# A two-layer transformer in one kernel: the first feed-forward's weights are dequantised inside the first attention

## The chip, the cores and the metric

The kernel runs on one core of a Trainium2 chip. The time is device microseconds of one execution. A core has TensorE (in the rows PE for matmuls, PEld for the loads of its stationary operand), VectorE (DVE), ScalarE (ACT), GpSimd (POOL) and SyncE (SP, which only issues transfers here), and 16 DMA engines. Each engine runs its own instructions in order; engines wait for each other by semaphores.

## The reference

Two layers, each an attention and a feed-forward, each followed by a residual addition and a layer norm. The sizes of layer 0, which the change touches:

- The input is 4 sequences of 256 tokens, 512 wide.
- Attention with latents: 32 heads; query latents of 192 (`c_q = h @ w_q_down`), key/value latents of 64, a rotated part of 64 per head. `q_lat = c_q @ w_q_up_nope @ w_uk` per head, scores from 64 latent and 64 rotated features, causal softmax, `out = probs @ c_kv @ w_uv`, then `@ w_out`.
- A feed-forward whose weights come in 4 bits, eight to a 32-bit word, with a zero and a scale for each group of 128 rows:

```python
def _dequant(qw, qz, sc, g_idx):
    wq = (qw[:, None, :] >> shifts) & 15            # 512 x 2752 and 1376 x 512 weights
    zq = ((qz[:, :, None] >> shifts) & 15) + 1.0    # 4 and 10 groups
    return sc[g_idx] * (wq - zq[g_idx])
h = silu(x @ w_gate) * (x @ w_up);  y = h @ w_d
```

Layer 1 has a grouped-query attention beside a latent one, and a feed-forward whose weights are quantised and dequantised by a 16-value code. The change leaves it alone.

## The kernel before

Everything is float32. A product is made of three matmuls of rounded parts (`product`: high x high, high x low, low x high; lines 63 to 65), so every operand is split into a high part (a rounding copy, mostly on ScalarE) and a low part (a subtraction, on VectorE or GpSimd).

The kernel is a row of blocks: `l0_attention_block`, `gptq_block` (which dequantises), `ffn_block`, and the same for layer 1. The order of the work in each engine's queue is written out by hand.

**First attention.** Four groups of 8 heads; a group is 16 steps, a step is one pair of heads of one sequence. Step n on TensorE: `scores(n)`; a query unit ("A", n+2) that makes the query features of the step after next; `apply(n-2)` (probabilities times values); `turn(n-1, 0)` (transposes); `output(n-3)`; `turn(n-1, 1)`; and in some steps a further unit: ("B", n) in steps 0 to 3 folds `w_uv` with `w_out`, ("W", n-12) in steps 12 to 15 folds the next group's `w_q_up_nope` with `w_uk`. Units write into a ring of two PSUM banks; `ring_free` counts those that have been emptied. The 192 query latents lie as 128 rows and 64 rows, so a query unit is, for each of two heads, three matmuls of 128 rows and three of 64 rows, 256 columns each (`project`, line 546).

Step n on VectorE: `peaks(n)` (the rows' maxima of the scores, line 766), `rotate` (lines 746 to 748), `shares` (the reciprocals, line 772), `probs_low(n-1, 0)` (line 777), `out_low(n-2)` (line 782), `probs_low(n-1, 1)`, in every fourth step `add_output` (line 790), and `plain_low` (line 758) for the B or W unit. ScalarE runs the exponentials, the scaling by the shares and the high parts; GpSimd adds the two halves of the rotation (line 366), splits the raw weights of the coming units (lines 351 and 359: two pieces in steps 0, 1, 2 and 15, one in 10 to 13) and makes the queries' low part (line 374). SyncE loads the raw weight pieces into two buffers, each once the split has freed it. Groups 1 and 2 are one loop body (`Fori`); groups 0 and 3 are written out.

**`gptq_block`.** After the attention, SyncE loads packed words, zeros, scales and group indices. VectorE makes one-hot tables of the group indices, unpacks the zeros and splits the scales (lines 1782 to 1805). Then 35 pieces of up to 512 columns: TensorE spreads zeros and scales over the rows with three matmuls, and VectorE shifts and masks the words (line 1816), subtracts the zeros (1821) and multiplies by the scales (1824) into `WGU` and `WD`, which stay in SBUF.

**`ffn_block`.** 22 units (11 tiles of the hidden width, twice for two halves of the tokens); ScalarE and GpSimd split each unit's weights from `WGU` and `WD`, TensorE multiplies.

Of the kernel before, what the change touches and what calls it, by code (L numbers as in the profile page):

```python
# [10 lines left out]
I32 = mybir.dt.int32  # L11
# [15 lines left out]
INTER = 1376  # L27
FT = 11
# [159 lines left out]
def l0_step_units(n, last):  # L188
# [8 lines left out]
    return out  # L197


def l0_units(first, last):  # L200

    out = [("W", i, 0) for i in range(PAIRS)] + [("A", 0), ("A", 1)] if first else []
    for n in range(L0_STEPS):
        out += l0_step_units(n, last)
    return out


def l0_attention_block(nc, x, X, XT, CQ, KC, CV, signals, norm, normed, ident, ident_d, banks, w_down, lat_cos_d, lat_sin_d,
                       w_nr, w_ou, cos_d, sin_d, mask_d):

    NP = 2
    with ExitStack() as ctx:
# [5 lines left out]
        QW = pair("qw", [P, PAIRS, NP, 2, P])  # L218
# [7 lines left out]
        mask = sb("mask", [P, P], F32)  # L226
        mask_r, ident_r = sb("mask_r", [P, P], R32), sb("ident_r", [P, P], R32)
        straight, crossed = sb("straight", [P, 2, HALF], F32), sb("crossed", [P, 2, HALF], F32)
        probs = sb("probs", [P, 2, NP * 3 * P], F32)
        dip, total, share = sb("dip", [P, 2, 4], F32), sb("total", [P, 2, 4], F32), sb("share", [P, 2, 4], F32)  # L230
        LN = QL + LAT + ROPE
        lat_raw, lat_w = sb("lat_raw", [P, KT, LN], F32), pair("lat_w", [P, KT, LN])
        lat_cos, lat_sin = sb("lat_cos", [P, SEQ], F32), sb("lat_sin", [P, SEQ], F32)
        lat_straight, lat_cross = sb("lat_straight", [P, 2, HALF], F32), sb("lat_cross", [P, 2, HALF], F32)
# [11 lines left out]
        lat_low, lat_ready = sem("lat_low"), sem("lat_ready")  # L246
        passed = {"pool": sem("passed_pool")}
        landed = [sem("landed0"), sem("landed1")]
        split_hi, split = sem("split_hi"), sem("split")
# [15 lines left out]
        def span(kind, first, last, g):  # L265

            lists = {"pieces": lambda f, l: [x for _, x in l0_pieces(f, l)], "units": l0_units,
                     "roped": lambda f, l: [u for u in l0_units(f, l) if u[0] == "A"],
                     "plain": lambda f, l: [u for u in l0_units(f, l) if u[0] in "WB"]}[kind]
            n0, n1 = len(lists(True, False)), len(lists(False, False))  # L270
            base = 0 if first else n0 + n1 * (g - 1)
            odd = 0 if first else n0
            names = lists(first, last)
            return {x: base + i for i, x in enumerate(names)}, {x: odd + i for i, x in enumerate(names)}

        assert len(l0_pieces(False, False)) % 2 == 0 and len(l0_units(False, False)) % 2 == 0
# [7 lines left out]
        def plain_cells(name, bank, x):  # L284

            i = name[1]
            if name[0] == "W":
                view = bank[:, 0:4 * LAT].rearrange("p (k h r) -> p k h r", k=2, h=NP)
                return [(x[0][:, i, :, 0, 0:LAT], view[:, 0]), (x[0][0:QP, i, :, 1, 0:LAT], view[0:QP, 1])]
            return [(x[1][:, i, :], bank[:, :])]  # L290
# [4 lines left out]
        def _(sp):  # L295
            sp.dma_start(ident[:, :], ident_d).then_inc(ident_landed, 16)
            for i in range(TT // 2):
                sp.dma_start(X[:, 2 * i:2 * i + 2, :], x[2 * i * P:2 * (i + 1) * P, :]
                             .rearrange("(t p) d -> p t d", p=P)).then_inc(x_landed[i], 16)
                if i == 0:  # L300
                    sp.dma_start(lat_raw[:, :, :], w_down.rearrange("(k p) m -> p k m", p=P)).then_inc(lat_landed, 16)
            sp.dma_start(lat_cos[:, :], lat_cos_d).then_inc(lat_landed, 16)
            sp.dma_start(lat_sin[:, :], lat_sin_d).then_inc(lat_landed, 16)
            sp.dma_start(cos[:, :], cos_d).then_inc(tables, 16)
            sp.dma_start(sin[:, :], sin_d).then_inc(tables, 16)
            sp.dma_start(mask[:, :], mask_d).then_inc(tables, 16)

            def body(g, first, last):
                at, place = span("pieces", first, last, g)
                for _, name in l0_pieces(first, last):  # L310
                    kind, i, h, ahead = name
                    slot = place[name] % 2
                    wait(sp, split, at[name] - 1)
                    if kind == "NR":
# [1739 lines left out]
```

## Time and profile before

| | |
|---|---|
| median of 3 runs | 2554.64 us (2553.92 to 2555.03) |
| the profiled execution | 2551.88 us, its span 2550.0 us |
| mean granted TensorE clock | 0.959 of 2.4 GHz |
| busy: TensorE, weight loads, VectorE, ScalarE, GpSimd | 92%, 80%, 69%, 57%, 62% of the span |
| first attention, its steps | 60 to 590 us |
| dequantisation | 590 to 685 us |
| first feed-forward | 685 to 885 us |

The span runs from the first to the last instruction. Busy shares are means over stages of different kinds, so the rows below go by stretches: length, then for each engine the busy time and (x) its instructions, then the granted clock (1.00 is 2.4 GHz, 0.50 is 1.2 GHz). A time line gives start, duration, engine, line, operation, output<-input, shape and count; in brackets is the idle time before it and what ended it.

### The profile page before, as it was taken

The page shows a single profiled execution, that of the slowest core. Times are in us where ns is not written, and L with a number is a line of the kernel's source. Part 1 is how long each engine was busy: PE and PEld are TensorE (multiplying, and loading weights), DVE is VectorE, ACT ScalarE, POOL GpSimd, SP SyncE. Part 2 cuts the span into 40 slices and gives each one's busy share as a digit, 9 for nine tenths or more (in the row PEclk, how much of TensorE's full clock was granted, in tenths as well). Part 3 has the DMA queues.
Part 4 walks back from the last instruction along what each step waited for, and adds up shares of the span by engine and source line. Part 5 has one row for each costly group of instructions (what it writes and reads, how often), then busy time and mean ns, then how long its engine had stood idle before and what let it go on. Part 6 is the DMA issues. An engine that isn't in the chain of part 4 may idle for free. (4 is left out here: it accounts for less than half of the span.)

```text
span 2550.0 us, 44356 instructions
## 1 busy us (share of the span) xinstructions
PE 2338.2 (92%) x14245; PEld 2027.7 (80%) x14245; DVE 1770.5 (69%) x3131; ACT 1459.0 (57%) x3978; POOL 1572.4 (62%) x1320
## 2 busy tenths in 40 slices
PE   7999999983899889999999999999999999987998
PEld 5788888872588778888888888888888888875886
DVE  4666666666823379888888888888888888972232
ACT  2666656660133347766666666676676766664432
POOL 3555555620154377877887878878878878751442
PEclk8999999995599999999999999999999999998999
DMA  2101110101000120110111111101101111003000
GB/s 97 32 28 36 28 36 23 29 1 41 1 1 1 35 67 29 52 54 16 56 45 37 52 38 48 51 19 57 50 24 56 37 47 48 18 5 141 1 17 17
DMA packets 41349, 93.70 MB, mean 37 GB/s; under 512 B 4836, under 2 KB 6760, under 8 KB 39808
## 3 DMA queue, kind: packets, MB, share of 16 engines
q1 hardware_dynamic: 41092, 90.55, 11.1%
q8 instruction: 128, 2.10, 0.4%
q14 instruction: 129, 1.06, 0.1%
HBM read 79.78 MB, written 10.75 MB: 36 GB/s over the span
## 5 line engine op out<-in xcount | busy, mean ns | idle before, releaser
L1129 POOL TENSOR_TENSOR a_nf_acc<-a_nf_acc,a_nf_term 128x512 f32<-128x512 f32 (+1 forms) x416 | 591.3, 1421 | 140.5 <-ACT a_nf_term L1223 70.1
L1609 POOL TENSOR_TENSOR f_w_lo<-WGU,f_w_hi 128x512 fp32r<-128x512 f32 x88 | 114.8, 1307 | 345.4 <-ACT f_w_hi L1625 345.2
L1183 ACT ACTIVATE a_probs<-bank,a_dip 128x128 f32<-128x128 f32 (+1 forms) x512 | 208.3, 419 | 191.5 <-DVE a_dip L1464 191.5
L1192 ACT ACTIVATE a_probs<-a_probs,a_share 128x128 f32<-128x128 f32 (+1 forms) x512 | 192.5, 464 | 68.7 <-DVE a_share L1470 68.7
L1110 POOL TENSOR_TENSOR a_qk_lo<-a_straight,a_qk_hi 128x512 fp32r<-128x512 f32 (+1 forms) x160 | 194.4, 1217 | 41.2 <-ACT a_qk_hi L1169 41.2
L63 PE MATMUL bank<-a_wo_hi,a_ot_hi 128*128 128x512 f32 x512 | 212.3, 415 | 0.0
L1475 DVE TENSOR_TENSOR a_pt_lo<-bank,a_pt_hi 128x384 fp32r<-128x384 f32 x256 | 140.8, 550 | 90.7 <-ACT a_pt_hi L1200 90.0
L1534 DVE TENSOR_SCALAR a_nf_term<-a_nf_unit 128x512 f32<-128x512 f32 (+1 forms) x288 | 199.7, 738 | 3.4 <-DVE a_nf_unit L1517 0.8
L65 PE MATMUL bank<-a_wo_hi,a_ot_lo 128*128 128x512 f32 x512 | 201.2, 393 | 0.0
L64 PE MATMUL bank<-a_wo_lo,a_ot_hi 128*128 128x512 f32 x512 | 200.8, 392 | 0.0
L1169 ACT ACTIVATE a_qk_hi<-a_straight 128x512 fp32r<-128x512 f32 (+1 forms) x160 | 94.4, 590 | 183.2 <-DVE a_straight L1449 183.2
L366 POOL TENSOR_TENSOR a_straight<-a_straight,a_crossed 128x512 f32<-128x512 f32 x64 | 82.5, 1289 | 182.6 <-DVE a_crossed L748 182.6
L1675 DVE TENSOR_TENSOR f_hidden<-bank,f_act_gate 128x512 f32<-128x512 f32 x44 | 30.4, 692 | 231.5 <-PE bank L65 213.8
L1338 PE MATMUL bank<-ident,a_probs 128*128 128x128 f32 x768 | 133.8, 284 | 52.5 <-DVE a_pt_lo L1475 52.5
L443 ACT ACTIVATE a_probs<-bank,a_dip 128x128 f32<-128x128 f32 (+1 forms) x256 | 104.2, 419 | 133.3 <-DVE a_dip L766 133.3
L63 PE MATMUL bank<-a_wvk_hi,XT_hi 128*128 128x320 f32 x512 | 170.8, 334 | 7.6 <-DVE a_crossed L1446 7.6
L1449 DVE TENSOR_TENSOR a_straight<-a_straight,a_crossed 128x512 f32<-128x512 f32 (+1 forms) x160 | 156.8, 980 | 5.5
L64 PE MATMUL bank<-a_wvk_lo,XT_hi 128*128 128x320 f32 x512 | 159.6, 312 | 0.0
L65 PE MATMUL bank<-a_wvk_hi,XT_lo 128*128 128x320 f32 x512 | 159.5, 312 | 0.0
L1338 PEld LDWEIGHTS bank<-ident,a_probs 128*128 128x128 f32 x768 | 85.4, 142 | 86.7 <-DVE a_pt_lo L1475 78.4
L63 PE MATMUL bank<-a_pt_hi,a_vl_hi 128*128 128x256 f32 (+1 forms) x512 | 137.8, 269 | 11.2 <-DVE a_pt_lo L1475 10.9
L63 PE MATMUL bank<-XT_hi,a_wql_hi 128*128 128x256 f32 x512 | 144.0, 281 | 0.0
(243 smaller groups left out, 8537.1 us busy)
## 6 DMA issues: line engine op xcount, KB each, us to landing
a_raw<-in_l_o SPq DMA_DIRECT2D x64, 256.0 KB, 2.7
a_raw<-in_l_vk SPq DMA_DIRECT2D x32, 384.0 KB, 3.1
a_raw<-in_l_ql SPq DMA_DIRECT2D x32, 320.0 KB, 2.9
a_raw<-in_l_ou SPq DMA_DIRECT2D x32, 288.0 KB, 2.8
n_codes<-coded_w SPq DMA_DIRECT2D x8, 1056.0 KB, 12.8
a_raw<-in_l_nr SPq DMA_DIRECT2D x16, 384.0 KB, 3.1
a_nf_raw<-in_w_nf SPq DMA_DIRECT2D x24, 256.0 KB, 2.6
coded_w<-a_nf_acc SPq DMA_DIRECT2D x24, 256.0 KB, 2.0
```

The source lines that it names most:

```text
L63: pe.matmul(out, lh, rh, start=first, stop=False)
L64: pe.matmul(out, lh, rl, start=False, stop=False)
L65: return pe.matmul(out, ll, rh, start=False, stop=last)
L1110: pool.tensor_tensor(rope_cell(name, QK.lo), src, rope_cell(name, QK.hi).bitcast(F32), ALU.subtract)\
L1129: pool.tensor_tensor(acc, left, nf_term[:, i % CODE_RING, 0:w], ALU.add).then_inc(nf_added, 1)
L1183: act.activation(probs[:, n % 2, col:col + keys], bank[:, at:at + keys], ACT.Exp, bias=dip[:, n % 2, i:i + 1], accum_out=total[:, n % 2, i ...
L1192: ins = act.activation(cell, cell, ACT.Copy, scale=share[:, n % 2, i:i + 1])
L1338: last_ = pe.transpose(TURN[:, i * P:(i + 1) * P], probs[:, n % 2, col:col + P], ident[:, :])
L1449: dve.tensor_tensor(row, row, crossed[:, 0:n], ALU.add).then_inc(rope_sum, 1)
L1475: dve.tensor_tensor(PT.lo[:, at], TURN[:, 0:3 * P], PT.hi[:, at].bitcast(F32), ALU.subtract)\
L1534: dve.tensor_scalar(nf_term[:, i % CODE_RING, 0:w], nf_unit[:, 0:w], -BOUNDS[k], JUMPS[k], ALU.is_ge, ALU.mult).then_inc(nf_terms, 1)
L1609: pool.tensor_tensor(lo, src, hi.bitcast(F32), ALU.subtract).then_inc(part_lo[i], 1)
```

## The change

- The first feed-forward's weights are dequantised inside the first attention, in 66 units of 256 columns, called ("G", i). They run from step 5 of group 0 to step 13 of group 3, one in each step, two in steps 6, 8 and 10 of groups 0 to 2. TensorE does two matmuls for a unit, with 128 rows: rows 0 to 31 hold zeros, rows 64 to 95 the scales' high part, rows 96 to 127 their low part, and two one-hot tables select zeros or scales. VectorE does shift, subtraction and multiplication at the end of its step. The result goes from one of three small buffers to DRAM.
- The preparation runs on VectorE in steps 0 to 3 of group 0, and a shift of the packed words in step 5.
- `gptq_block` is gone. `ffn_block` loads each unit's three weight tiles from DRAM; ScalarE waits for them.
- The query latents 128 to 191 lie twice in the second row block (rows 0 to 63 and 64 to 127 of it), their low part beside zeros, and the second block of the folded weight holds its high part over its low part. Two matmuls of 128 rows take the place of three of 64.
- Groups 1 and 2 are written out instead of being a loop; the loads of raw pieces are issued at stated steps.

```diff
+DEQ_WIDE, DEQ_UNITS = 44, 66
+DEQ_FIRST = 5
+DEQ_TWICE = [(g, n) for g in range(3) for n in (6, 8, 10)]
...
         def groups(eng, body):
             body(0, True, False)
-            with eng.Fori(1, L0_GROUPS - 1) as g:
+            for g in range(1, L0_GROUPS - 1):
                 body(g, False, False)
...
+            def store(i):
+                src = parked[:, i % 3, :]
+                sp.wait_ge(dequantised, i + 1)
...
+                sp.dma_start(dst, src).then_inc(q_stored[i % 3], 16)
...
+                    if first and n == 3:
+                        sp.wait_ge(q_ready, 1)
+                        sp.dma_start(packed, q["q_gu"]).then_inc(q_landed, 16)
+                        sp.dma_start(packed_d, q["q_d"]).then_inc(q_landed, 16)
+                    for _, i in dequantised_at(g, n):
+                        store(i)
...
-                            product(pe, out, QW[:, i, h, 0, :], CQ[:, 0, at], True, False)
-                            last_ = product(pe, out, QW[0:QP, i, h, 1, :], CQ[0:QP, 1, at], False, True)
+                            product(pe, out, (QW_both[:, i, h, 0, :], QW_lo[:, i, h, :]), CQ[:, 0, at], True, False)
+                            pe.matmul(out, QW_both[:, i, h, 1, :], CQ.hi[:, 1, at], start=False, stop=False)
+                            last_ = pe.matmul(out, QW_both[:, i, h, 1, :], CQ.lo[:, 1, at], start=False, stop=True)
...
+                    elif name[0] == "G":
+                        pe.wait_ge(q_ready, 1)
...
+                        pe.matmul(bank[:, 0:PART], hot_zero[:, rows:rows + P], table[:, cols:cols + PART],
+                                  start=True, stop=True)
+                        last_ = pe.matmul(bank[:, PART:2 * PART], hot_scale[:, rows:rows + P], table[:, cols:cols + PART],
+                                          start=True, stop=True)
...
+                def dequantise(names):
+                    for name in names:
...
+                        wait(dve, differed, i - 1)
+                        dve.tensor_scalar(nib[:, i % 2, :], src, shift, 15, ALU.logical_shift_right, ALU.bitwise_and)\
+                           .then_inc(nibbled, 1)
+                    for name in names:
...
+                        dve.wait_ge(nibbled, i + 1)
+                        dve.wait_ge(unit_done, number[name] + 1)
+                        wait(dve, dequantised, i - 1)
+                        dve.tensor_tensor(diff[:, i % 2, :], nib[:, i % 2, :], bank[:, 0:PART], ALU.subtract)\
+                           .then_inc(differed, 1)
+                    for name in names:
...
+                        dve.wait_ge(differed, i + 1)
+                        wait(dve, q_stored[i % 3], 16 * (i // 3))
+                        dve.tensor_tensor(parked[:, i % 3, :], diff[:, i % 2, :], bank[:, PART:2 * PART], ALU.mult)\
+                           .then_inc(dequantised, 1)
+                        dve.wait_ge(dequantised, i + 1)
+                        dve.sem_inc(ring_free, 1)
...
                     for name in units:
-                        if name[0] != "A":
+                        if name[0] in "WB":
                             plain_low(name)
+                    if first and n < 4:
+                        (zeros_out, scales_high, scales_low, groups_hot)[n]()
+                    if first and n == DEQ_FIRST:
+                        odd_words_shifted()
+                    dequantise([name for name in units if name[0] == "G"])
...
+                if source and u < FT:
+                    act.wait_ge(loaded[u], 48)
...
+            if source:
+                for m in range(FT):
+                    for i in range(2):
+                        sp.dma_start(WGU[:, :, (i * FT + m) * P:(i * FT + m + 1) * P], source[0][i * FT + m])\
+                          .then_inc(loaded[m], 16)
+                    sp.dma_start(WD[:, m, :], source[1][m]).then_inc(loaded[m], 16)
...
-def gptq_block(nc, ident, banks, WGU, WD, q):
```

`zeros_out`, `scales_high`, `scales_low`, `groups_hot` and `odd_words_shifted` hold the instructions of the old block's preparation (the zeros' shifts; copies and the plus one; the scales' low part; two pairs of one-hot tables; the shifts of the packed words), over 32 to 128 partitions, each set closed by a wait for its own end.

## Rows read from the trace of the kernel before

**Rows 1.** Busy time by stretch: length, PE, PEld, DVE, ACT, POOL, PEclk, DMA, GB/s.
```profile
60.45:187.90 127.45, 122.25 (x826) 105.91 (x826) 81.51 (x159) 81.17 (x264) 68.14 (x76) 0.97 0.09 28
187.90:318.90 131.00, 128.32 (x874) 109.98 (x873) 84.52 (x164) 82.72 (x268) 74.60 (x85) 1.00 0.12 34
318.90:450.47 131.57, 131.56 (x874) 112.91 (x874) 84.53 (x165) 82.83 (x268) 68.31 (x76) 0.97 0.10 28
450.47:589.84 139.37, 128.33 (x834) 109.81 (x832) 88.95 (x176) 82.72 (x264) 53.11 (x57) 0.96 0.05 14
589.84:690.70 100.86, 57.86 (x121) 31.81 (x122) 83.26 (x155) 4.20 (x9) 2.63 (x3) 0.51 0.08 26
690.70:885.00 194.30, 188.58 (x828) 152.75 (x828) 54.67 (x89) 72.08 (x122) 83.00 (x64) 1.00 0.03 8
```

**Rows 2.** Time line at the entry of the first feed-forward: start, duration, engine, instruction.
```profile
685.60 0.63 ACT L1625 ACTIVATE f_w_hi<-WGU 128x512 fp32r<-128x512 f32 x1 [100.38 <-PEq L1733]
...
690.70 0.50 PE L63 MATMUL bank<-XT_hi,f_w_hi 128*128 128x512 f32 x1 [1.41 <-DVE XT_lo L145]
```

**Rows 3.** DMA issues of the page: count, size, median time to landing.
```profile
a_raw<-in_l_o SPq DMA_DIRECT2D x64, 256.0 KB, 2.7
```

**Rows 4.** Time line of TensorE in a plain step of group 1.
```profile
252.37 0.28 PE L63 MATMUL bank<-CQ_hi,a_qw_hi 128*128 128x256 f32 x1
...
252.61 0.28 PE L65 MATMUL bank<-CQ_hi,a_qw_lo 128*128 128x256 f32 x1
...
252.82 0.38 PE L63 MATMUL bank<-CQ_hi,a_qw_hi 64*128 64x256 f32 x1
...
254.46 0.38 PE L63 MATMUL bank<-a_pt_hi,CV_hi 128*128 128x256 f32 x1
...
259.74 0.28 PE L63 MATMUL bank<-CQ_hi,a_qw_hi 128*128 128x256 f32 x1
```

**Rows 5.** Time line of VectorE in the late step of group 3.
```profile
509.28 0.99 DVE L766 TENSOR_REDUCE a_dip<-bank 128x2 f32<-128x256 f32 x2
...
514.54 0.56 DVE L777 TENSOR_TENSOR a_pt_lo<-bank,a_pt_hi 128x384 fp32r<-128x384 f32 x1 [0.95 <-ACT a_pt_hi L460]
```

**Rows 6.** Time line of VectorE: two shifts of 256-column pieces.
```profile
661.81 0.29 DVE L1816 TENSOR_SCALAR q_nib<-q_packed 128x256 uint32<-128x256 uint32 x1
...
662.92 0.28 DVE L1816 TENSOR_SCALAR q_nib<-q_packed 128x256 uint32<-128x256 uint32 x1
```

**Rows 7.** Time line of VectorE and GpSimd behind the probabilities' low part.
```profile
204.57 0.69 DVE L758 TENSOR_TENSOR a_bh_lo<-bank,a_bh_hi 128x512 fp32r<-128x512 f32 x1 [0.74 <-ACT a_bh_hi L433]
...
305.29 0.56 DVE L777 TENSOR_TENSOR a_pt_lo<-bank,a_pt_hi 128x384 fp32r<-128x384 f32 x1 [1.01 <-ACT a_pt_hi L460]
305.76 1.28 DVE L790 TENSOR_TENSOR X<-bank,X 128x512 f32<-128x512 f32 x2
305.85 1.29 POOL L374 TENSOR_TENSOR a_q_lo<-a_straight,a_q_hi 128x512 fp32r<-128x512 f32 x1 [1.54 <-ACT a_q_hi L428]
306.96 0.47 DVE L758 TENSOR_TENSOR a_qw_lo<-bank,a_qw_hi 128x128 fp32r<-128x128 f32 x2
```

**Rows 8.** Busy time in the preparation of the dequantisation, columns as in rows 1.
```profile
606.09:625.06 18.97, 1.54 (x4) 1.24 (x5) 18.69 (x39) 0.00 (x0) 0.00 (x0) 0.50 0.00 0
```

**Rows 9.** Time line of GpSimd and VectorE, then one tile's instruction (min/median/max) and its group.
```profile
18.36 1.27 POOL L359 TENSOR_TENSOR a_wn_lo<-a_raw,a_wn_hi 128x512 fp32r<-128x512 f32 x1
18.41 1.30 DVE L695 CAST a_mask_r<-a_mask 128x128 fp32r<-128x128 f32 x1
...
L1534 DVE TENSOR_SCALAR a_nf_term<-a_nf_unit x288: 411/454/1983, 919.3 to 2290.4; 128x512 f32<-128x512 f32 x112, 128x576 f32<-128x576 f32 x32
...
L1534 DVE TENSOR_SCALAR a_nf_term<-a_nf_unit 128x512 f32<-128x512 f32 (+1 forms) x288 | 199.7, 738 | 3.4 <-DVE a_nf_unit L1517 0.8
```

**Rows 10.** TensorE at the loop's jump back, then the stretch behind it.
```profile
316.51 0.32 PE L63 MATMUL bank<-KC_hi,a_q_hi 128*128 128x128 f32 x1 [2.63 <-issue]
...
319.00:322.00 3.00, 3.00 (x12) 2.33 (x10) 0.92 (x2) 1.72 (x8) 0.00 (x0) 0.50 0.23 81
```

More of the change, by code:

```diff
@@ L27 @@
 INTER = 1376
+Q_GROUPS = (D // 128, INTER // 128)
 FT = 11
@@ L265, in span, with plain_cells @@
         def span(kind, first, last, g):
[L267 to L276, printed above, removed]
+            names = {"pieces": lambda k: [x for _, x in l0_pieces(k == 0, k == L0_GROUPS - 1)], "units": l0_units,
+                     "tails": lambda k: [x for _, x in l0_pieces(k == 0, k == L0_GROUPS - 1) if x[0] == "NR"],
+                     "roped": lambda k: [u for u in l0_units(k) if u[0] == "A"],
+                     "plain": lambda k: [u for u in l0_units(k) if u[0] in "WB"]}[kind]
+            base = sum(len(names(k)) for k in range(g))
+            at = {x: base + i for i, x in enumerate(names(g))}
+            return at, at
         def groups(eng, body):
             body(0, True, False)
-            with eng.Fori(1, L0_GROUPS - 1) as g:
+            for g in range(1, L0_GROUPS - 1):
                 body(g, False, False)
             body(L0_GROUPS - 1, False, True)
-        def plain_cells(name, bank, x):
+        def plain_cells(name, bank):
             i = name[1]
@@ L328, in body @@
                 number, _ = span("units", first, last, g)
+                tails, _ = span("tails", first, last, g)
                 def split_piece(name):
@@ L389, in body @@
                 for n in range(L0_STEPS):
-                    own = [name for name in l0_step_units(n, last) if name[0] == "A"]
+                    own = [name for name in l0_step_units(g, n) if name[0] == "A"]
                     for name in own:
@@ L541, in piece_ready @@
                     else:
-                        names = [x for _, x in l0_pieces(False, False)]
-                        left = len(names) - names.index((kind, i, h, 1))
-                        pe.wait_ge(split, pieces[("OU", 1, 0, 0)] - left + 1)
+                        pe.wait_ge(split, span("pieces", g == 1, False, g - 1)[0][(kind, i, h, 1)] + 1)
                 def project(name):
@@ L650, in body @@
                     scores(n)
-                    units = l0_step_units(n, last)
+                    units = l0_step_units(g, n)
                     for name in units:
@@ L804, in body @@
                 for n in range(L0_STEPS):
-                    units = l0_step_units(n, last)
+                    units = l0_step_units(g, n)
                     peaks(n)
@@ L1588, in ffn_block @@
         UNITS = 2 * FT
+        loaded = [sem(f"loaded{m}") for m in range(FT)] if source else None
         late = range(TT - 2, TT)
```

377 lines of the change are left out of this document (205 added, 172 removed).

## The prediction

> **What bounds the kernel now.** I read the sums by stretch first [rows 1]. The first attention runs in four head groups of 16 steps. TensorE is busy 122 to 132 us in each of them (VectorE 82 to 89), and its clock is at 2.4 GHz (granted 0.96 to 1.00). So TensorE sets the time there. The fifth stretch, 100.86 us long, is the dequantisation. There VectorE is busy 83 us and the clock is at 1.2 GHz (0.51). The time line of the two ends of that stretch gives its price [rows 2]: the attention's last addition ends at 589.84, and the first product with a dequantised weight starts at 690.70. Then I followed one step on TensorE [rows 4], one step in which VectorE came late [rows 5], and the dequantisation of a 256-column piece [rows 6], because these decide what a step costs once pieces are in it.
>
> **The removed stage.** 100.86 us go. In their place the feed-forward must fetch its first three weight tiles (256 KB each, issued 0.3 to 0.5 us apart). A 256 KB load of this kernel lands after 2.7 us [rows 3]; written in 512-byte pieces I take 3.5, so about 4.7 us until ScalarE may start. From its first weight copy to the first product were 5.1 us (685.60 to 690.70 [rows 2]); TensorE's transposes are done by then, so I take 4.7. Sum 9.4. Before, the clock was back at 1.00 there [rows 1]; after a wait of this length it will start at 1.2 GHz, and a first stretch like the one at 319 to 322 (0.50) [rows 10] costs some 2.3 us. 100.9 - 11.7 = **89.2 us saved**. Every further load has a unit of 8.8 us to arrive in (22 units in the 195 us to 885 [rows 1]), so it is hidden.
>
> **TensorE in a step.** A plain step takes 7.37 us (252.37 to 259.74), of which the query unit takes 2.09 [rows 4]. Its matmuls stand 0.12 apart (two spacings from 252.37 to 252.61), but a change between 128 and 64 rows costs more: the first 64-row one starts 0.21 behind 252.61, and the one behind it is late as well. Twelve spacings would be 1.44, so the four changes take the other 0.65. Ten matmuls of 128 rows take 1.20, and 0.10 behind the last change goes too. The dequantisation unit adds two matmuls, 0.24. Without the register-addressed loop the plain step was 7.29 already (groups 0 and 3). New: 7.29 - 0.89 - 0.10 + 0.24 = **6.54 us**. If TensorE stayed the bound, 64 steps would give back some 45 us.
>
> **VectorE in a step.** It won't stay the bound. VectorE's queue is in order, and a step is a chain through ScalarE and back. The late step shows it with no wait for TensorE [rows 5]: maxima at 509.28, second half of the probabilities' low part at 514.54, 5.26 later, and after another 0.48 the queue is free (305.29 to 305.76 [rows 7]): 5.74 us. In other steps the rotation waited about 1 us longer for the query unit; the shorter unit takes that wait away. Behind the chain now comes the dequantisation: three instructions of 0.29, 0.42 and 0.42 us, 1.11 from one piece's start to the next [rows 6], and 0.11 for the wait that now stands behind the multiplication: **1.22 us**, in line before the next maxima. So a plain step is 6.96, VectorE's and not TensorE's. Two units cost 2.0. Every fourth step adds 1.20 for the residual (305.76 to 306.96 [rows 7]). A step with an output-weight unit waits for ScalarE and ends its low part at 7.23 (it starts 0.56 + 0.74 = 1.30 us behind the probabilities' start [rows 7]; 0.05 for the ring and 0.62 for itself), in all 8.45; one with a folded query weight 7.8.
>
> A middle group: steps 0 to 3 are 3 x 8.45 + 8.78 = 34.1; steps 4 to 11 are 13.9 + 8.95 + 7.2 + 7.75 + 7.2 + 8.95 + 7.2 = 61.2; steps 12 to 15 are 3 x 7.8 + 8.55 = 31.95. Sum **127.2**, against 131.0 and 131.6 [rows 1]. Half of that difference is the loop's jump back, which goes: TensorE idled 2.63 us at 316.51 and then ran at 1.2 GHz [rows 10]. So -3.8 and -4.4. Group 3 by the same step prices over its first 14 steps: 109.2 against 110.2, **-1.0**; its tail has no units.
>
> **Group 0** carries the preparation. Before it ran from 606.09 to 625.06 on VectorE, 19.0 us [rows 8]; with a second pair of one-hot tables (1.4) and three tail shifts (1.4) it is 22 us: 3.6, 3.9, 3.7 and 7.8 in steps 0 to 3 and 3.0 in step 5. VectorE's slack there is 1.2 to 1.5 per step, so steps 0 to 3 get longer by 2.2, 2.0, 2.9 and 6.4, steps 4 and 5 together by 2.0, and steps 6 to 15 by 2.3 in sum (the unit prices above against the old lengths): 17.8. TensorE idles several us at a time here, more than the 2.63 us before the drop of rows 10, and comes back at 1.2 GHz: +2. The packed words (2.4 MB) are asked for at the end of step 3 and needed 12 us later. The old stage began its preparation 16.2 us after its own start, with all its loads landed before [rows 1, 8]; a wait of a few us here is in the range, none is in the sum. The lead-in gains 1 us by two shorter query units. **+19**.
>
> **A price that hides in no instruction's own length.** The shift reads and writes SBUF at two elements a cycle's worth (0.285 us for 256 columns). A copy of that kind, 128x128, took 1.30 us at 18.41, exactly as long as GpSimd's subtraction from 18.36 was running, and TENSOR_SCALAR of 128x512 in the second attention, which has GpSimd working beside it nearly all the time, averages 0.738 (0.411 to 1.983, median 0.454) [rows 9]. So a shift can cost 0 to 1.29 us more (one whole GpSimd subtraction); the mean of that row lies 0.33 above its least. I go through the step: GpSimd splits weights behind the rotation in steps 0 to 2, 10 to 13 and 15 and is caught in the middle of an instruction (0.4 to 0.5 each, 19 steps with units); in two-unit steps the second shift loses its turn; in plain steps the shift would stand where the residual starts at 305.76, 0.09 ahead of GpSimd's query subtraction at 305.85 [rows 7]. Taken 66 x 0.30 = **+20**, and +4 for the preparation, whose copies are of the same kind.
>
> That GpSimd and VectorE exclude one another is a rule of the Trainium skill (SBUF — State Buffer, "Who interferes with whom"): whoever issues first holds the shared port pair for its whole instruction, and the other blocks. By that rule the 0.09 us in the plain steps decide; the trace agrees in the copy of rows 9.
>
> **Sum.** -89.2 - 3.8 - 4.4 - 1.0 + 19 + 24 = -55.4. The profiled execution took 2551.88 (span 2550.0 and 1.9 around it), so 2496.5; the median of the runs is 2.8 above it: **2499 us**. Stores of the results (128 KB each, three buffers, so three steps for some 2.5 us) and SP's queue, in which each store stands behind the loads of its step, I cost at nothing: the next load needs that step's split anyway. If that cover went, a load would come up to a step late, some 3 us in each of 8 pairs.
>
> **Rivals.**
> A. The shift loses its race in the plain steps too, and waits out the 1.29 us less the lead: 21 steps by some 1.15 us more, +24: 2523. For: only 0.09 us of lead. Against: ScalarE's order fixes it, and a late ScalarE only helps. 0.20.
> B. No port price: -24: 2475. For: half of the instructions in the tile's row take no more than 0.454, GpSimd or not. Against: the copy in the same rows. 0.17.
> C. VectorE's work fits in its idle time (1.0 us waiting for ScalarE in each step before the second low part [rows 5]), and TensorE stays the bound: groups shorter by 12, 12, 12 and 8 more, no port price: 2431. Against: the dequantisation stands behind that wait, not in it. 0.06.
> D. Slower: TensorE's idle time between steps brings the clock down to 1.2 GHz within the attention. Its 6.54 us of work become some 13, a step grows by 5 to 6 us, and from 10 such steps of 64 the 55 us are eaten; all of them give some 2850. For: after 2.63 us of idling it fell [rows 10]. Against: the new gaps are 0.4 us in plain steps, and TensorE's clock was 1.00 in the first middle group (busy 128.3 of 131.0 [rows 1]). 0.03.
>
> **Numbers.** My forecast 0.54 (2485 to 2512 by itself), the rivals as given. Range 2465 to 2530: it holds B and A and leaves out C and D and a preparation that costs much more. What this measurement can tell from no change is 0.2%, 5 us: faster 0.96, same 0.01, slower 0.03.
>
> **What would show it.** Right: no idle 100 us; VectorE without idle before its maxima, TensorE waiting 0.3 to 0.5 us a step; plain steps near 7.0; step 3 of group 0 near 15; shifts of 0.28 beside some of 0.7 to 1.5. Wrong: plain steps at 6.5 (C) or 8.1 (A), a granted clock near 0.5 in groups 1 to 3 (D), a first product later than 15 us behind the last addition.

## The result and the profile after

| | before | changed |
|---|---|---|
| median (4 runs each on one chip) | 2554.28 us (2550.14 to 2555.03) | 2517.30 us (2512.97 to 2518.66) |
| profiled execution, its span | 2551.88, 2550.0 | 2517.41, 2515.6 |
| mean granted TensorE clock | 0.959 | 0.962 |

The ratio is 0.9856 (95% interval 0.9839 to 0.9873): 37 us faster, where 55 were forecast. The time by stretch (the four groups, the entry of the feed-forward), columns as in [rows 1]:

```profile
58.51:223.50 164.99, 124.94 (x820) 114.42 (x819) 126.11 (x245) 79.06 (x264) 76.75 (x82) 0.84 0.15 47
223.50:359.58 136.08, 120.68 (x878) 109.28 (x878) 106.91 (x221) 79.61 (x268) 72.97 (x85) 0.97 0.17 48
359.58:495.77 136.19, 121.06 (x878) 109.89 (x878) 106.98 (x221) 79.86 (x268) 73.03 (x85) 0.97 0.17 48
495.77:640.89 145.12, 124.46 (x834) 111.83 (x834) 103.08 (x218) 80.81 (x264) 53.09 (x55) 0.93 0.09 27
640.89:651.31 10.42, 2.98 (x16) 2.61 (x17) 4.30 (x10) 3.98 (x9) 2.74 (x3) 0.56 0.83 247
```

Beside [rows 1]: the 100.86 us stretch has become one of 10.42; group 0 is 37.5 us longer, groups 1 and 2 are 5.1 and 4.6, group 3 with its tail 5.8. TensorE is busy for less time than before in groups 1 to 3 (120.7 us against 128.3 in group 1) and idles 15 us in a middle group; VectorE is busy 22 us more there.

VectorE and GpSimd at the end of a plain step (what was [rows 7]). The shift starts 0.09 us ahead of GpSimd's subtraction and takes 0.28. The subtraction and the multiplication behind it run beside that GpSimd instruction and take their usual 0.42:

```profile
271.29 0.56 DVE L929 TENSOR_TENSOR a_pt_lo<-bank,a_pt_hi 128x384 fp32r<-128x384 f32 x1 [0.94 <-ACT a_pt_hi L545]
271.76 0.28 DVE L950 TENSOR_SCALAR a_lat_in<-a_q_wide 128x256 uint32<-128x256 uint32 x1
272.08 0.42 DVE L958 TENSOR_TENSOR a_lat_in<-a_lat_in,bank 128x256 f32<-128x256 uint32 x1
272.54 0.42 DVE L965 TENSOR_TENSOR a_lat_in<-a_lat_in,bank 128x256 f32<-128x256 f32 x1
273.10 0.42 DVE L918 TENSOR_REDUCE a_dip<-bank 128x2 f32<-128x256 f32 x1
...
271.85 1.34 POOL L453 TENSOR_TENSOR a_q_lo<-a_straight,a_q_hi 128x512 fp32r<-128x512 f32 x1 [1.46 <-ACT a_q_hi L510]
```

Two-unit step 10 of group 1, VectorE, GpSimd and TensorE. The two shifts take 2.13 us and end when the second of GpSimd's instructions does (within 0.15 us): both are waited out (such a wait is called a lock below). TensorE stands 3.48 us at the first matmul of the next query unit, whose ring bank the first multiplication empties:

```profile
312.64 2.13 DVE L950 TENSOR_SCALAR a_lat_in<-a_q_wide 128x256 uint32<-128x256 uint32 x2
...
312.09 1.26 POOL L438 TENSOR_TENSOR a_wn_lo<-a_raw,a_wn_hi 128x512 fp32r<-128x512 f32 x1
313.31 1.31 POOL L453 TENSOR_TENSOR a_q_lo<-a_straight,a_q_hi 128x512 fp32r<-128x512 f32 x1
...
315.88 0.58 PE L64 MATMUL bank<-CQ_hi,a_qw_both 128*128 128x256 f32 x1 [3.48 <-DVEq L968]
```

The sums by stretch of a plain step, of step 10 and of step 11. In step 11 the clock is 0.75, TensorE is busy throughout, and the step takes 9.82 us:

```profile
266.00:273.10 7.10, 6.68 (x52) 6.08 (x52) 5.67 (x12) 4.72 (x16) 2.63 (x3) 1.00 0.07 21
...
305.68:316.54 10.86, 6.95 (x50) 6.14 (x50) 9.29 (x17) 4.72 (x16) 5.77 (x8) 0.91 0.17 52
316.54:326.36 9.82, 9.82 (x62) 9.43 (x62) 6.51 (x12) 4.87 (x16) 5.60 (x7) 0.75 0.12 32
```

Group 0, steps 0 to 3, in the same view; then VectorE and TensorE in them. In steps 0 to 2 VectorE idles 2 us and more for ScalarE's copy of the output weight, and only then do the preparation's instructions come; TensorE idles up to 10.86 us, and its clock is 0.65 to 0.74 (1.00 in step 3):

```profile
58.51:72.66 14.15, 7.30 (x43) 6.65 (x42) 10.27 (x32) 4.22 (x14) 7.47 (x10) 0.74 0.15 43
72.66:86.60 13.94, 9.09 (x48) 8.27 (x48) 10.06 (x13) 5.20 (x16) 8.80 (x10) 0.65 0.16 43
86.60:99.44 12.84, 8.71 (x49) 8.13 (x49) 9.24 (x13) 5.48 (x17) 9.43 (x10) 0.73 0.10 31
99.44:114.80 15.36, 9.38 (x62) 7.95 (x60) 12.98 (x21) 5.36 (x17) 3.67 (x3) 1.00 0.09 27
```

```profile
76.67 0.90 PE L697 MATMUL bank<-ident,a_probs 128*128 128x128 f32 x3 [10.86 <-DVE a_pt_lo L929]
...
80.79 0.69 DVE L910 TENSOR_TENSOR a_bh_lo<-bank,a_bh_hi 128x512 fp32r<-128x512 f32 x1 [2.11 <-ACT a_bh_hi L515]
81.40 1.73 DVE L854 TENSOR_SCALAR XT_hi<-a_q_wide 32x2816 fp32r<-32x2816 uint32 x1
```

The entry of the feed-forward (what was [rows 2]): last addition, first weight copy, first product.

```profile
639.60 1.29 DVE L975 TENSOR_TENSOR X<-bank,X 128x512 f32<-128x512 f32 x2
...
647.33 0.63 ACT L1818 ACTIVATE f_w_hi<-WGU 128x512 fp32r<-128x512 f32 x1 [11.06 <-DMA WD<-deq_d]
...
651.31 0.79 PE L64 MATMUL bank<-XT_hi,f_w_hi 128*128 128x512 f32 x1 [7.13 <-DVE XT_lo L146]
```

### The profile page after: what moved, and what is told of

It is laid out like the page before. It is cut to its first block and busy times, and to the rows that moved or that the text cites. A ratio compares the mean times of both kernels' runs of the same rounds, so it can differ in the third digit from the quotient of the medians.

```text
span 2515.6 us, 43939 instructions
## 1 busy us (share of the span) xinstructions
PE 2265.2 (90%) x14144; PEld 2008.6 (80%) x14144; DVE 1791.2 (71%) x3230; ACT 1450.9 (58%) x3980; POOL 1585.0 (63%) x1336
## 5 line engine op out<-in xcount | busy, mean ns | idle before, releaser
L64 PE MATMUL bank<-XT_hi,f_w_hi 128*128 128x512 f32 x352 | 140.1, 398 | 9.4 <-DVE XT_lo L146 9.4
```

Of the source, the lines that this page charges most:

```text
L64: pe.matmul(out, lh, rh, start=first, stop=False)
```

## The experiments

Each was timed beside the kernel before, and the ratio is to that; a difference between two of the new kernels is taken from their ratios (0.0010 is 2.55 us), since they ran beside different runs of before. A step's length below is the distance between the starts of VectorE's first maxima of two steps. Here are the steps of group 1, in the changed kernel and in the three others that tell most. Group 2 of the changed kernel has the same sum, but 8.09 in step 9 and 8.89 in step 11:

| step | 0 | 1 | 2 | 3 | 4 | 5 | 6 | 7 | 8 | 9 | 10 | 11 | 12 | 13 | 14 | 15 | sum |
|---|---|---|---|---|---|---|---|---|---|---|---|---|---|---|---|---|---|
| before, unrolled | 8.67 | 8.65 | 8.67 | 8.67 | 7.29 | 7.29 | 8.03 | 6.54 | 7.29 | 7.27 | 8.04 | 6.53 | 8.31 | 8.30 | 8.42 | 8.18 | 126.2 |
| changed | 9.24 | 8.63 | 8.89 | 8.63 | 7.11 | 7.10 | 9.26 | 7.11 | 9.11 | 7.10 | 10.86 | 9.82 | 8.10 | 8.11 | 8.91 | 8.10 | 136.1 |
| early shift | 8.83 | 8.31 | 8.57 | 8.31 | 6.78 | 6.80 | 8.81 | 6.78 | 7.65 | 6.78 | 8.82 | 6.78 | 7.79 | 7.79 | 8.61 | 7.77 | 125.2 |
| no VectorE work | 8.10 | 8.10 | 8.10 | 8.27 | 6.72 | 6.71 | 7.71 | 6.76 | 6.95 | 6.72 | 7.71 | 6.77 | 7.73 | 7.72 | 8.07 | 7.83 | 120.0 |

**The shift, moved forward** (`shift_early`).

```diff
                         out_low(n - 2)
+                    nibbles(deq)        # the shifts of this step's units; step 5 of group 0 as before
                     probs_low(n - 1, 1)
...
                     dequantise(deq)     # subtraction and multiplication
```

> The shift of a unit's words stands ahead of the probabilities' second low part, where VectorE idles 0.94 us in a plain step (270.35 to 271.29 in the trace after), and no longer at the step's end. Theory Q (VectorE's queue at the end of a step sets its length, and a shift caught behind a GpSimd instruction is paid there, then again as TensorE's wait for the ring and as a lower clock): plain steps 7.10 -> 6.8, the two-unit step 8 9.11 -> 7.9, step 10 10.86 -> 9.0, step 11 9.82 -> 7.4; total 2475 to 2485. Rival L (only the 0.28 us of the shift itself leaves the queue, locks cost nothing behind themselves): 66 x 0.30 = 20, total 2497. Rival M (GpSimd's rotation sum and splits run in just that gap, so the shift is caught there, delays the low part and TensorE's transposes): 2517 or more.

Measured: 2479.17 us (2475.36 to 2481.50), ratio to before 0.9723 (0.9706 to 0.9739), 34 us below the changed kernel; from trace to trace the attention ends 39.2 us earlier (last addition's start 600.45 against 639.60). The steps are those forecast by theory Q within 0.25 us but for step 11, which gained more (6.78). Here are the shifts of the two-unit step 8 of group 1, in VectorE's idle time ahead of the low part, for 0.50 us together. They start 0.14 us before GpSimd's rotation sum ends (277.71 for 1.28), so there is next to nothing to wait out:

```profile
278.85 0.50 DVE L950 TENSOR_SCALAR a_lat_in<-a_q_wide 128x256 uint32<-128x256 uint32 x2
279.90 0.56 DVE L929 TENSOR_TENSOR a_pt_lo<-bank,a_pt_hi 128x384 fp32r<-128x384 f32 x1 [0.54 <-ACT a_pt_hi L545]
```

Moving an instruction of 0.28 us was worth 34 to 39 us over 65 places (the shift in step 5 of group 0 stayed): 0.32 us in a plain step, 1.46 in step 8, and 5.1 in steps 10 and 11 together, where the lock, the long wait for the ring and the lower clock went with it. Rival L's 20 us, the instruction's own length, are the larger part of that; the rest is priced by the kernels that follow. Rival M falls: the longest shift is now 0.70 us.

**Is it the port?** Two kernels put another instruction of 256 columns in the shift's place. First `shift_one_port`:

```diff
-  dve.tensor_scalar(nib, src, shift, 15, logical_shift_right, bitwise_and)
+  dve.tensor_tensor(nib, same, same, subtract)     # same: 256 columns of SBUF
```

> In the place of the shift stands a TENSOR_TENSOR subtraction of 256 float32 columns, SBUF to SBUF (it leaves out the unpacking of the weights). By the trace such an instruction takes 0.42 us, not 0.28. Theory P (the long shifts of 1.0 to 1.6 us are the port shared with GpSimd, held by GpSimd's whole instruction, and two-input instructions don't wait for it): all 66 take 0.4 to 0.45 us, none over 0.6; plain steps 7.10 -> 7.24, step 8 9.11 -> 8.4, step 10 10.86 -> 9.3, step 11 9.82 -> 8.0; 10 us of excess go, 9 us of length come, and TensorE's stall and clock in steps 10 and 11 give 5 to 10: total 2507 to 2513. Rival R (they were late for a reason other than the port, such as the SBUF traffic of GpSimd or DMA): instructions of over 1 us stay in steps 8 to 11, total 2525 or more.

Measured: 2528.34 us, ratio 0.9915 (0.9898 to 0.9931). The times are the rival's, and long instructions stayed. But the test didn't tell the two causes apart: P took it that an instruction with two SBUF inputs doesn't wait, and that could be wrong by itself. The second kernel, `shift_from_psum`, reads PSUM instead:

```diff
+  dve.tensor_scalar(nib, bank[:, 0:PART], 1.0, None, mult)     # bank: PSUM
```

> The changed kernel, order as it is; in the place of the shift stands a one-input TENSOR_SCALAR of 256 columns that reads the unit's zeros from PSUM and writes SBUF (it leaves out the unpacking; the weights become zeros). Theory P (a VectorE instruction waits for GpSimd's when it needs the SBUF port that they share; both the shift, SBUF to SBUF in one input, and the two-input SBUF subtraction tried earlier, with its longest at 1.50, need it; one that reads PSUM does not): all 66 take about 0.42 us, none over 0.6; plain steps 7.10 -> 7.24, step 8 9.11 -> 8.4, step 10 10.86 -> 9.4, step 11 9.82 -> 8.0 or less: total 2507 to 2513. Rival R (any VectorE instruction that starts while GpSimd is inside one is late, or its write is what waits): some stay over 1 us, as 1.50 in the SBUF subtraction, total 2525 to 2530 like that one.

Measured: 2514.23 us, ratio 0.9857 (0.9840 to 0.9873). All 66 instructions of each kernel by tile (min/median/max ns): the changed kernel's shifts in two rows and its subtraction (one input in SBUF, one in PSUM), then the SBUF subtraction, then the PSUM copy:

```profile
L950 DVE TENSOR_SCALAR a_lat_in<-a_q_wide x44: 280/294/1372, 133.1 to 431.6; 128x256 uint32<-128x256 uint32 x44
L950 DVE TENSOR_SCALAR a_lat_in<-a_lat_turn x22: 261/285/1346, 441.5 to 610.0; 128x256 uint32<-128x256 uint32 x22
L958 DVE TENSOR_TENSOR a_lat_in<-a_lat_in,bank x66: 405/421/423, 133.4 to 610.3; 128x256 f32<-128x256 uint32 x66
```

```profile
L951 DVE TENSOR_TENSOR a_lat_in<-XT_hi x66: 391/418/1502, 132.4 to 619.6; 128x256 f32<-128x256 f32 x66
```

```profile
L951 DVE TENSOR_SCALAR a_lat_in<-bank x66: 407/415/425, 133.0 to 606.4; 128x256 f32<-128x256 f32 x66
```

In the same place, beside the same GpSimd instructions, reading PSUM leaves no long one. So what waits is an instruction all of whose inputs lie in SBUF, one input or two. A read from SBUF alone isn't enough: the subtraction in line 958 has one input there and one in PSUM, often runs beside GpSimd, and never took more than 0.423 us. The Trainium skill (SBUF — State Buffer, "Who interferes with whom") names two kinds of VectorE instruction that exclude GpSimd's: those in a 2-port mode, which `tensor_scalar` can enter, and those with two SBUF inputs, these only against a GpSimd instruction that reads SBUF; these runs agree (0.425 us at most from PSUM, 1.37 and 1.50 from SBUF). Steps 8, 10 and 11 of group 1 went to 8.28, 9.48 and 7.23, within 0.1 us of P's forecast or below it; the total is 1 us above P's range and far below R's. Over all 66 the instruction is 0.13 us longer (8.6 us), and the attention ends 3.5 us earlier all the same (last addition's start 636.09 against 639.60). So the locks on the shifts had cost some 12 us, 11.0 of it in the shifts' own lengths (44 at a mean of 0.480 and 22 at 0.398 make 29.9 us; 66 at 0.285 would be 18.8). Of the 34 us that the early shift brought, then, some 12 are locks and most of the rest is the shift's own length, gone from the end of the queue.

**No VectorE work in the units** (`no_vector_work`).

With a memset of the buffers in step 5, and in each unit:

```diff
-  shift, subtraction, multiplication
+  dve.wait_ge(unit_done, number[name] + 1)
+  dve.memset(nib[0:1, i % 2, 0:1], 0).then_inc(dequantised, 1)
```

> Units keep TensorE's two matmuls and the store; VectorE's shift, subtraction and multiplication are left out (the weights are zeros), one memset of an element stands for them; the preparation stays. Theory Q (VectorE's queue is the bound of nearly all steps with units): plain steps 7.10 -> 6.7 (TensorE's 6.68 of work), steps 6, 8, 10 and 11 to 6.8 to 7.0, TensorE's clock 1.00 throughout groups 1 to 3; groups 1 and 2 some 117 to 119 us each (from 136), group 3 some 8 us shorter, group 0 some 14: total 2455 to 2465. Rival T (TensorE or ScalarE bounds the steps, units are nearly hidden): above 2500.

Measured: 2460.50 us, ratio 0.9649 (0.9632 to 0.9666); groups 1 and 2 take 120.0 each (117 to 119 expected), a plain step 6.72 with TensorE busy for 6.68 of it:

```profile
241.85:248.57 6.72, 6.68 (x52) 6.08 (x51) 4.73 (x11) 4.76 (x16) 1.87 (x2) 1.00 0.06 20
```

VectorE's part of the units cost the changed kernel 53 us, 34 of them by the place of the shift. Rival C of the prediction would have needed all of this to be hidden, and even this kernel is 29 us above its 2431.

**The query unit with 64 rows again**, on the changed kernel (`rows64`) and on that with the early shift (`rows64_early`):

```diff
-  pe.matmul(out, QW_both[:, i, h, 1, :], CQ.hi[:, 1, at], ...)
-  last_ = pe.matmul(out, QW_both[:, i, h, 1, :], CQ.lo[:, 1, at], ...)
+  three matmuls on rows 0 to 63: (QW_both, CQ.hi), (QW_both, CQ.lo), (QW_both, CQ.hi)
```

> The query unit's second row block goes back to three matmuls of 64 rows (the third repeats the first's operands, so the weights' low part is left out there). Theory Q: TensorE's work in a plain step goes from 6.68 to some 7.5 us and it becomes the bound there: plain steps 7.10 -> 7.5; steps 6, 8, 10 and 11, where VectorE is 2 us late, keep their length; over 60 steps some 15 to 25 us: total 2532 to 2542. Rival S (TensorE has enough idle time in every step, the rows' change bought nothing): 2517 to 2522. Rival F (the full 0.99 us in each of 64 steps): 2580.

> The kernel with the early shift, with the query unit's second row block in three matmuls of 64 rows again (the third repeats the first's operands). Theory Q (now that VectorE's queue is short, TensorE's longer step shows in full in plain steps, and without the clock's drops of the run on the changed kernel, since its long stalls for the ring are gone): plain steps 6.78 -> 7.52, step 8 7.65 -> 7.9, steps 0 to 3 and 12 to 15 +0.4 to 0.7; some 8 to 9 us a group: total 2510 to 2515. Rival C (the 43 us that the 64 rows cost on the changed kernel were mostly clock drops behind two-unit steps, and these return): above 2520, with steps 7, 9 and 11 over 9 us.

Measured: 2560.36 us, ratio 1.0046 (1.0030 to 1.0063), and 2537.99, ratio 0.9934 (0.9912 to 0.9956). Both lie above theory Q, though its plain steps came out (7.45 to 7.53), and the first fits none of its rivals. Of the second run's rival C the total and steps 7 and 11 hold (11.75 and 10.21 in group 1); step 9 stayed at 7.48. Step 6 (two units) and step 7 of group 1, first with 64 rows and the early shift, then the early shift alone:

```profile
276.31:285.85 9.54, 8.03 (x54) 6.99 (x54) 7.81 (x17) 4.95 (x16) 2.93 (x3) 0.97 0.06 16
285.85:297.61 11.76, 11.76 (x54) 10.17 (x52) 5.67 (x13) 4.98 (x16) 2.19 (x2) 0.59 0.07 22
```

```profile
258.99:267.80 8.81, 7.26 (x55) 6.46 (x54) 7.64 (x17) 4.72 (x16) 2.96 (x3) 1.00 0.05 16
267.80:274.58 6.78, 6.57 (x51) 5.97 (x50) 5.58 (x13) 4.72 (x16) 2.21 (x2) 1.00 0.14 41
```

In both TensorE had stood for the ring late in step 6 (1.5 and 1.43 us). With 128 rows it went on at 2.4 GHz (1.00); with 64 rows the next step averaged 0.59, so for most of it TensorE was at 1.2 GHz, and the step took 5 us longer. The rows alone don't decide that, nor does the stop's length alone. The changed kernel, all with 128 rows, stops for 1.73 us at the same place of groups 1 and 2, behind step 8, and step 9 then runs at 1.00 in one group and at 0.83 in the other:

```profile
297.91 0.39 PE L64 MATMUL bank<-CQ_hi,a_qw_both 128*128 128x256 f32 x1 [1.73 <-DVEq L968]
298.58:305.68 7.10, 6.87 (x54) 6.28 (x53) 5.67 (x12) 4.72 (x16) 2.53 (x2) 1.00 0.12 37
...
434.04 0.58 PE L64 MATMUL bank<-CQ_hi,a_qw_both 128*128 128x256 f32 x1 [1.73 <-DVEq L968]
434.71:442.80 8.09, 8.09 (x55) 7.70 (x55) 5.77 (x12) 4.84 (x16) 2.54 (x2) 0.83 0.12 34
```

In group 1 of the kernel with the early shift the 64 rows cost 18.1 us (143.3 against 125.2): 6.9 in steps 7 and 11 beyond the 0.74 of a plain step, 11.2 by their own length. In all, the change of rows was worth 49 us to the changed kernel and 54 with the early shift.

**No preparation** (`no_preparation`).

```diff
-  (zeros_out, scales_high, scales_low, groups_hot)[n]()      # steps 0 to 3
+  if n == 3: dve.sem_inc(q_ready, 1)
-  odd_words_shifted()                                        # step 5
+  dve.wait_ge(q_landed, 32)
```

> The changed kernel with the preparation's VectorE instructions left out (zeros, scales, one-hot tables, the shift of the odd words; the tables hold other data, so the weights are not the right ones); the waits for the loads stay where step 5 has them. Theory Q (each preparation instruction stands in VectorE's queue behind the wait for ScalarE's copy of the output weight, so it adds its whole length): steps 0 to 3 56.3 -> about 36 us as before the change, step 5 11.64 -> 7.2 to 8, TensorE's clock 1.00 in group 0, groups 1 to 3 unchanged (136.1, 136.2): total 2489 to 2494. Rival W (the loads of 2.4 MB of packed words hold step 5 and later ones, and the B units set steps 0 to 3): total 2503 or more.

Measured: 2482.33 us, ratio 0.9735 (0.9719 to 0.9752); steps 0 to 5 7.74, 9.90, 7.86, 7.88, 6.48, 7.39 against 14.15, 13.94, 12.84, 15.36, 8.00, 11.64, in all 28.7 us, and 2.6 in the ten steps behind them. The preparation costs 31 us in group 0, and 31 by the ratios: more than theory Q gave it (23 to 28). In the changed kernel its instructions fill 27 us of VectorE's queue in steps 0 to 3 and 5, so none of it was hidden. The loads of the words (rival W) don't hold the kernel: step 5, with the wait for them, takes 7.39.

**Preparation ahead of the output-weight unit's low part** (`preparation_ahead`, on the early shift).

```diff
+                    if first and n < 4:
+                        (zeros_out, scales_high, scales_low, groups_hot)[n]()
                     for name in units:
                         if name[0] in "WB":
                             plain_low(name)
```

> The kernel with the early shift, and in steps 0 to 3 the preparation ahead of the low part of the output-weight unit, where VectorE idles 2.57, 2.11, 2.11 and 0.74 us for ScalarE. Theory Q (VectorE's queue sets these steps too, the idle time there is usable): steps 14.15, 13.93, 12.83, 15.36 get 2.1 to 2.6 (the last 0.7) shorter, 7.5 us in sum: against the kernel with the early shift 2472, or 0.9695 of before. Rival V (the preparation meets GpSimd's splits there, and the locks eat what the idle time gives): 2479 or more.

Measured: 2476.43 us, ratio 0.9711 (0.9695 to 0.9727): 3 us instead of 7.5, both by the ratios, whose intervals overlap, and in group 0 of the traces (150.3 us against 153.3). Steps 1 and 2 gained 2.5 and 2.0 (11.44, 10.86); steps 5 and 7 together lost 1.4; step 0 gained nothing (14.06). There the small shifts met more of GpSimd's instructions and were some 2 us longer in all (VectorE; L846 takes 0.19 and L848 0.21 elsewhere):

```profile
63.52 0.61 DVE L846 TENSOR_SCALAR a_q_wide<-a_lat_in 32x88 uint32<-32x88 uint32 x1
64.05 0.21 DVE L848 TENSOR_SCALAR a_lat_in<-a_lat_turn 32x64 uint32<-32x64 uint32 x1
...
64.53 1.28 DVE L848 TENSOR_SCALAR a_lat_in<-a_lat_turn 32x64 uint32<-32x64 uint32 x1
```

So Q and V each hold in some steps.

**Units first** (`units_first`, on the one before).

```diff
     out.append(("A", n + 2))
+    out += dequantised_at(g, n)        # ahead of ("B", n) and ("W", n - 12, 1)
...
+                    dequantise(deq)    # ahead of plain_low
```

> As the one before, and in steps 0 to 3 and 12 to 15 the dequantisation unit stands ahead of the output-weight or query-weight unit on TensorE, and its subtraction and multiplication ahead of that unit's low part on VectorE (idle time there: 0.76 and 0.3 us). Theory Q: steps 0 to 3 of groups 1 to 3 from 8.3 to about 8.1, where TensorE sets them (8.10 without VectorE's work), steps 12, 13 and 15 7.78 -> 7.73: 24 steps, 3 us in all: 2469. Rival: no gain, TensorE waits for the ring instead.

Measured: 2473.09 us, ratio 0.9702 (0.9684 to 0.9719). Groups 1 and 2 went from 125.1 to 124.4 each (steps 0 to 3: 8.35, 8.09, 8.85, 7.90): 1.5 us of the 3 are seen there. The intervals of the two kernels overlap.

**Second units side by side** (`doubles_together`, on the early shift): `n in (7, 8, 9)` for `(6, 8, 10)`.

> The kernel with the early shift, with the nine second units in steps 7, 8 and 9 of groups 0 to 2, not in 6, 8 and 10. Theory Q (a second unit is 0.85 us of VectorE's queue wherever that queue sets the step): steps 6 and 10 8.81 -> 7.96, steps 7 and 9 6.78 -> 7.65, sums of the groups within 0.3 us, total 2478 to 2480. Rival (what a second unit costs is the wait for its ring bank, worse when such steps follow each other, or better away from the residual's addition): sums differ by more than 1 us per group.

Measured: 2481.65 us, ratio 0.9729 (0.9715 to 0.9744); groups 1 and 2 took 125.13 and 125.50 against 125.22 and 125.24; steps 7, 8, 9 of group 1 are at 7.62, steps 6 and 10 at 7.97. A second unit was 0.85 us of VectorE's queue in each of the places tried.

**The loop of the kernel before, written out** (`before_unrolled`).

```diff
-            with eng.Fori(1, L0_GROUPS - 1) as g:
+            for g in range(1, L0_GROUPS - 1):
```

> The kernel before, with groups 1 and 2 of the first attention written out instead of looped. Theory: the stop of 2.6 us at the jump back, the lower clock behind it (3.3 us in the last step of group 1, 3.8 in the first of group 2) and 0.09 in each plain step go: step 15 of group 1 11.55 -> 8.2, step 0 of group 2 12.65 -> 8.8, the rest of the 32 steps some 2 us in sum: 8 to 9 us less than before, ratio 0.9965. Rival: straight code brings waits for instructions in the same places, ratio 0.999 to 1.001.

Measured: 2546.24 us, ratio 0.9981 (0.9971 to 0.9991): 4 to 5 us, some half of the forecast. In the trace the attention did get 10.6 us shorter (last addition at 577.95, 588.56 before), but the second attention, whose code is the same, took 1379.5 us from its first to its last maxima and not 1373.2. The trace is of the slowest of this kernel's ten runs, 5 us above their median, so part of that may belong to this one execution.

**All that paid, and one thing more** (`tiles_first`): at the entry of the feed-forward ScalarE copies the first four token tiles and then waits for weights.

```diff
-            split_high(0, 0)
             for t in range(HT):
                 high_tile(act, XT, banks[t], signals, flipped, t)
+            split_high(0, 0); split_high(0, 1)
```

> All edits that paid (early shift, preparation ahead, units first), and at the feed-forward's entry ScalarE makes the high parts of the first four token tiles before it waits for the first weight tiles (so far it waits 10.9 us for the loads with these copies behind the wait, and TensorE's first product waits for VectorE's low part of them). Theory: the copies are done while the loads are under way; the first product starts some 7.5 us behind the last addition's end and not 10.3: 3 us less than the kernel without this edit, 2469 to 2470, ratio to before 0.9685. Rival: the loads bound the entry anyway (256 KB in 512-byte pieces, 5.4 us each with all in flight): under 1 us.

Measured: 2469.18 us (2467.15 to 2476.97), ratio 0.9676 (0.9662 to 0.9689). This beats both kernels, before by 3.2% (83 us) and the changed one by 46 us. The first product comes 8.4 us behind the last addition's end (598.76), not 10.3: 1.9 us of the 3. By the ratios it is 7 us below the kernel before it, but the intervals overlap, and the trace shows no more than these 1.9 at the entry. ScalarE waits for the loads after the copies, too; now they bound the entry:

```profile
599.84 1.66 ACT L138 ACTIVATE XT_hi<-bank 128x512 fp32r<-128x512 f32 x3 [5.69 <-PE bank L130]
...
605.06 1.15 ACT L1828 ACTIVATE f_w_hi<-WGU 128x512 fp32r<-128x512 f32 x2 [2.71 <-DMA WD<-deq_d]
```

## Why the prediction was right in kind and 18 us short

The sign, the bound (VectorE's queue) and the saving at the removed stage held, and 2517.3 lies in the range of 2465 to 2530. It lies outside the 2485 to 2512 that the forecast gave itself, and the nearest number is rival A's 2523; but A's mechanism did not come (plain steps of 7.10 us, not 8.1), so the number alone would have pointed to the wrong cause. From profile to profile -34.5 us were measured, -55.4 forecast. By the prediction's own terms:

- **The removed stage, -89.2.** From the last addition to the first product 10.42 (9.4 forecast); behind it the feed-forward took 0.8 us longer (2.3 for the clock forecast): -89.6. The sum is right, in part by luck: ScalarE's first weight copy came 6.4 us behind the last addition (4.7 forecast), the first product 4.0 behind the copy (4.7), and the clock cost less than forecast.
- **TensorE's plain step, 6.54.** 6.68 in the trace, 6.72 as the bound without VectorE's work; with 64 rows 7.52 (the prediction's own terms give 7.53). Right within 0.15. (64 steps at 0.75 us are 48 us and not 45; no sum uses it.)
- **VectorE's plain step, 6.96.** 7.10. The race at the shift went as forecast, by the 0.09 us; rival A is out.
- **Groups 1 and 2, -3.8 and -4.4 with 5.7 each for the port.** Measured +5.1 and +4.6, 3.2 us too little in each. The step that failed: "Two units cost 2.0", taken as the whole price of a two-unit step. As VectorE's own time it was right (`doubles_together` has 0.85 for the second unit). Steps 6, 8, 10 and 11 were to take 32.9 us and 2.1 for the port; they took 39.1 (9.26, 9.11, 10.86, 9.82). In steps 8 and 10 the second shift loses its turn, as forecast, and in step 10 the first does too. What was left out is what hangs on it: the next query unit's bank is freed only behind all of this, TensorE stands up to 3.48 us, and its clock averaged 0.75 in the step behind. `shift_from_psum` has no locks on the shifts and runs the four steps of group 1 in 34.5 us, 33.6 without its longer instruction; so locks and what hangs on them cost 5.5 us there, 2.1 forecast, of which the shifts' own lengths are 3.5. (That kernel's group 1 as a whole gains only 1.5 us: the instruction is longer in every step, and step 7 runs at a clock of 0.79 and takes 8.28.) Early shifts took 1.5, 2.0 and 3.0 us from steps 8, 10 and 11. The gain from the loop was put at half of 8.2 us; it was 10.3 in these groups, so with the loop they would stand at 141.
- **Group 3, -1.0 and 4.2.** Measured +5.8, which is 2.5 more. The trace has two stops of TensorE of 3.13 us behind the steps that also measure the norm (1.1 us before the change), with a clock of 0.71 to 0.94 in the steps there. That these are the 2.5 us is not shown; no run took them apart.
- **Group 0, +19 and 4 for ports.** Steps 0 to 5 got 25.4 us longer, 21.8 forecast (15.5, 2, 4 and 0.3); steps 6 to 15 12.1, 6.2 forecast. The first is the slack of "1.2 to 1.5 per step" (the prediction's own figures take 1.9 in step 1 and 0.8 in step 2): the idle time stands ahead of the output-weight unit's low part, the preparation behind it, so the preparation's 27 us hid nowhere (28.7 by `no_preparation`), and moving it took 2.5 and 2.0 us from steps 1 and 2. What the clock of 0.65 to 0.74 cost beside that, where 2 us were forecast, no run took apart. Of the 5.9 us missing in the others 2.6 go with the preparation; 3.3 are of the size that groups 1 and 2 miss each.
- **The port, 66 x 0.30 = 20.** The mean was too high: 11.0 us in the instructions' own lengths, 12 in all, about halfway between the forecast and rival B (no port price). What hangs on a lock stood in no term.
- **The second attention, at nothing.** 1377.9 us against 1373.2: +4.7, in one execution of each. Whether the change did it is open.

The missing 21 us are 9.0 in groups 1 to 3, 8.6 in group 0 with its lead-in, and 4.7 in the second attention, less 1 elsewhere. Rivals C and D didn't come, though D's mechanism did on a small scale (0.75 to 0.83 in single steps of groups 1 and 2).

## What to carry to other kernels

On an engine that works in order, ask of an added instruction not only how long it is but what it stands behind and ahead of: 0.28 us put into a gap instead of behind it, 65 times, was worth 34 us of 2517. Where a helper unit shares a ring of buffers with the main work, price the case in which it comes twice by following the other engine's next claim on that ring. An idle time counts as slack only for instructions that are ahead of the wait in the queue.

## What the runs showed of the hardware

- A VectorE instruction whose inputs all lie in SBUF and that started inside a GpSimd instruction lasted until about that one's end: up to 1.37 us for 256 columns with one input, up to 1.50 with two. One that reads PSUM never did: 66 of 66 at 0.407 to 0.425, and 66 of 66 at 0.423 at most where the other input lay in SBUF.
- Behind a stop of TensorE of 1.5 us the granted clock averaged 0.59 over the next step in one kernel; behind one of 1.43 us at the same place it stayed at 1.00 in another, whose query units are shorter. In the changed kernel stops of 1.73 us at the same place of two groups were followed by 1.00 and 0.83. What decides is open.
- The second attention, whose code no kernel here changes, took 1373.2 us before, 1377.9 in the changed kernel and 1374.2 to 1379.8 in the other twelve, in one execution of each. In six of 32 places of the changed kernel a VectorE instruction starts 0.45 us behind the one that it follows, where it had been 0.20 (first a place before, then the same after):

```profile
1141.59 0.17 DVE L1512 SCALAR_TENSOR_TENSOR a_nf_safe<-a_nf_top 128x8 f32<-128x8 f32 x1
1141.79 0.20 DVE L1515 RECIPROCAL a_nf_inv<-a_nf_safe 128x8 f32<-128x8 f32 x1
...
1103.78 0.17 DVE L1702 SCALAR_TENSOR_TENSOR a_nf_safe<-a_nf_top 128x8 f32<-128x8 f32 x1
1104.23 0.20 DVE L1705 RECIPROCAL a_nf_inv<-a_nf_safe 128x8 f32<-128x8 f32 x1 [0.28 <-DVE a_nf_safe L1702]
```

That is 1.5 us of the 4.7 at most, and the unrolled kernel before, 6.3 us longer here, has none of it. What moved the stage is open; no run here tells.
